# A three-layer decoder on one core, with the steps of its five queues in another order

## The reference

```python
x = x + _L0_attn_ref(_layernorm(x, axis=-1), L0_attn_wq, L0_attn_wk_down, L0_attn_wv_down, L0_attn_wk_up, L0_attn_wv_up, L0_attn_wo)
x = x + _L0_xattn_ref(_layernorm(x, axis=-1), ctx_768, L0_xattn_Wq, L0_xattn_bq, ...)
x = x + _L0_ffn_ref(_layernorm(x, axis=-1), L0_ffn_w1, L0_ffn_b1, L0_ffn_w2, L0_ffn_b2)
...
# feed-forward: bitlinear, exact gelu, bitlinear, where bitlinear(x, w, b) is
xn = rmsnorm(x)
xq = activation_quant(xn)      # scale 127 / max|xn|, round, clip
wq = weight_quant(w)           # scale 1 / mean|w|, round, clip to -1, 0, 1
return einsum('bsi,oi->bso', xq, wq) + b
```

## Time and profile before

| | |
|---|---|
| median of 3 runs | 320.35 us (320.17 to 320.55) |
| the profiled execution, its own time | 321.1 us |
| its span in the trace | 319.2 us |
| PE busy | 302.6 us, 95% |
| DVE busy | 273.2 us, 86% |
| ACT busy | 191.0 us, 60% |
| POOL busy | 161.5 us, 51% |

### The profile page before, as it was taken

How to read it: one execution, slowest core, us unless ns; L and a number is a source line. 1 busy time by engine, 2 the same in 40 slices (tenths; PEclk the granted TensorE clock), 3 DMA queues, 4 the chain that set the end, 5 groups by cost and what they waited for, 6 DMA issues and landing times.

```text
span 319.2 us, 8883 instructions
## 1 busy us (share of the span) xinstructions
PE 302.6 (95%) x3185; PEld 248.8 (78%) x3198; DVE 273.2 (86%) x488; ACT 191.0 (60%) x369; POOL 161.5 (51%) x315
## 2 busy tenths in 40 slices
PE   8798999999999999999999999999999999998756
PEld 8476787879888887897788878887887888786534
DVE  2228996898989799999999999989999998999973
ACT  3164435436247759478966854497445965776852
POOL 7337006282933523671778266306660485077873
PEclk9899999999999999999999999999999999999978
DMA  7999000000000000000001010000000010000011
GB/s 200 340 368 330 6 3 0 2 2 0 4 2 2 3 0 2 3 0 2 2 3 34 3 35 2 2 0 4 16 18 2 2 37 2 0 3 33 3 34 66
DMA packets 11954, 12.54 MB, mean 39 GB/s; under 512 B 1668, under 2 KB 11144, under 8 KB 11912
## 3 DMA queue, kind: packets, MB, share of 16 engines
q1 hardware_dynamic: 10648, 11.40, 10.9%
q10 hardware_dynamic: 1264, 0.59, 0.7%
HBM read 9.89 MB, written 2.10 MB: 38 GB/s over the span
## 4 chain that ended last, share of the span: by engine, by line
PE 77%; issue 6%; DVE 6%; POOL 5%; ACT 5%; DVEq 0%; POOLq 0%; ACTq 0%
PE bank L1724 8%; PE bank L1871 7%; PE bank L1804 6%; PE bank L1894 6%; PE bank L1822 6%; PE bank L1903 5%; PE quad L1784 4%; PE bank L1885 4%; PE bank L1730 4%; PE quad L1861 3%; PE bank L1942 3%; PE bank L1757 3%; PE bank L1718 2%; PE bank L1923 2%; PE bank L1932 2%
## 5 line engine op out<-in xcount | busy, mean ns | idle before, releaser
L845 ACT ACTIVATE c_p<-bank 77x512 f32<-77x512 f32 x64 | 35.7, 591 | 26.4 <-PE bank L1871 26.2
L1871 PE MATMUL bank<-ident,c_s 128*77 128x128 f32 x256 | 34.8, 274 | 0.4 <-DVE f_o L1369 0.4
L564 POOL TENSOR_SCALAR f_s<-f_mv 128x1 f32<-128x1 f32 x16 | 3.5, 220 | 62.0 <-DVE f_s L1325 61.4
L821 ACT ACTIVATE a_p<-bank 128x512 f32<-128x512 f32 x48 | 27.3, 601 | 10.5 <-PE bank L1804 10.1
L1894 PE MATMUL bank<-c_y,xw_s 128*128 128x128 f32 x256 | 31.5, 276 | 0.8 <-DVE c_y L1303 0.8
L1871 PEld LDWEIGHTS bank<-ident,c_s 128*77 128x77 f32 x256 | 29.5, 148 | 3.1 <-issue 1.0
L1894 PEld LDWEIGHTS bank<-c_y,xw_s 128*128 128x128 f32 x256 | 30.1, 192 | 1.3 <-issue 0.9
L1903 PE MATMUL bank<-xw_s,c_h 128*128 128x256 f32 x128 | 30.5, 381 | 0.0
L1273 DVE TENSOR_REDUCE c_nm<-quad 128x16 f32<-128x1232 f32 x16 | 23.0, 1436 | 4.2 <-PE quad L1861 4.1
L1903 PEld LDWEIGHTS bank<-xw_s,c_h 128*128 128x128 f32 x128 | 23.3, 190 | 3.6 <-ACT c_h L854 0.5
L1284 DVE TENSOR_TENSOR c_s<-quad,c_nm 128x616 f32<-128x616 f32 x32 | 24.5, 792 | 1.3
(11 more groups left out here) (139 smaller groups left out, 769.8 us busy)
## 6 DMA issues: line engine op xcount, KB each, us to landing
out<-f_o SPq DMA_DIRECT2D x16, 128.0 KB, 1.7
xres<-in_x SPq DMA_DIRECT2D x1, 1536.0 KB, 10.0
c_p<-in_wqT SPq DMA_DIRECT2D x2, 512.0 KB, 6.9
c_p<-in_wo SPq DMA_DIRECT2D x1, 1024.0 KB, 9.6
f_h<-in_fw1T SPq DMA_DIRECT2D x1, 1024.0 KB, 12.1
c_s<-in_fw2T SPq DMA_DIRECT2D x1, 1024.0 KB, 11.3
xw_s<-in_xw SPq DMA_DIRECT2D x2, 512.0 KB, 9.7
fb_s<-in_fb SPq DMA_DIRECT2D x1, 512.0 KB, 6.3
```

The lines of the kernel that those rows point to most:

```text
L821: nc.scalar.activation(dst, src, ACT.Exp, scale=SCALE_SA).then_inc(sa.sem["act"], 1)
L845: nc.scalar.activation(c_p[0:M, :, qt * P:(qt + 1) * P].rearrange("p (c j g) t -> p c j g t", c=KC, g=Q2)[:, :, j, :, :], bank("xs", f"tr{ ...
L1871: last = nc.tensor.transpose(dst[0:M, g * P:(g + 1) * P], c_s[:, qt, j, g, :], ident[:, :])
```

## The change

The change is in the order alone. Every step, every tile and every transfer is there as before, but the queues of all five engines list them in another order: the rows of `ORDER`, the calls at the end of each block, the list `EMPTIED` and SP's sixteen stores. The program's table was searched for with every hand-over between two engines taken longer than it was measured. The table's rows say little to a reader; here are its first ones on PE, and one piece each of what follows from it.

```diff
--- before.py
+++ after.py
@@ ORDER (one of its rows per engine) @@
 ORDER = dict(
     pe="""
-        pro.v3.0 pro.v1.0 pro.v2.0 sp.xT.0 pro.wq0.0 pro.wq1.0 pro.wqk0.0 pro.k1.0 pro.wqk1.0 sp.k.0 sp.q.0 sp.xT.1
-        sa.suA.0 pro.v0.0 pro.k3.0 sp.k.1 sp.v.0 sa.suB.0 pro.wvo.0 sp.xT.2 sp.q.1 sa.trA1.0 sa.trA0.0 sp.k.2
...
+        pro.wq0.0 sp.xT.0 pro.wq1.0 pro.wqk0.0 pro.v3.0 pro.wqk1.0 sp.k.0 sp.q.0 pro.v2.0 pro.k3.0 sa.suA.0 pro.k2.0
+        pro.k1.0 pro.v1.0 sp.v.0 sa.suB.0 sp.xT.1 sa.trA1.0 sa.trA0.0 pro.v0.0 sp.q.1 sp.k.1 sa.trB0.0 sa.trB1.0
...
@@ EMPTIED: the same pairs, in the order in which PE first comes to them @@
-    ("pro", "v3"): ("dve", ("v3",)),
-    ("pro", "v1"): ("dve", ("v1",)),
-    ("pro", "v2"): ("dve", ("v2",)),
+    ("pro", "wq0"): ("act", ("wq0",)),
     ("sp", "xT"): ("act", ("xT",)),
-    ("pro", "wq0"): ("act", ("wq0",)),
...
@@ SP's stores @@
+            f2_store(0, 1)
             f2_store(0, 0)
-            f2_store(0, 1)
...
@@ POOL's calls @@
+            xp_rstd(0)
+            xp_norm(0)
             sp_rstd(3)
             sp_norm(3)
-            xp_rstd(0)
-            xp_norm(0)
```

More of the change, by code:

```diff
@@ L173 @@
[L173 to L176 removed]
+        sp.norm1.1 sp.veps.2 sp.rstd.2 sp.norm0.2 sp.norm1.2 xp.veps.0 xp.rstd.0 xp.norm0.0 xp.norm1.0 sp.veps.3
@@ L177 @@
+        f2.hr0.7 f2.ht0.7 f2.ham0.7 f2.hinv0.7 f2.hqs0.7 f2.ms1.7 f2.hr1.7 f2.ht1.7 f2.ham1.7 f2.hinv1.7 f2.hqs1.7
+        f1.fb2.7 f2.hsc0.7 f2.hsc1.7
     """,
```

1561 lines of the change are left out of this document (780 added, 781 removed).

## The result

The new order takes 325.96 us (median of 4 runs, 325.31 to 326.80), before took 320.45 (320.17 to 322.09) beside it: ratio 1.0163, 95% interval 1.0121 to 1.0204. It is 5.5 us slower; I had forecast 1.4 us slower and a range that ended at 324.6. The profiled execution is 325.86 us long with a span of 323.9, so 4.7 us of span against the 319.2 of before have to be found.

The account below looks back on a forecast made before the run. PE paces the middle, DVE the fourteen us from 290, a chain of short steps the last fifteen. 2.4 - 0.6 - 2.65 + 1.72 - 0.3 + 0.84 = +1.4 us on 320.35 gives 321.7 us; range 318.4 to 324.6.

Parts of the forecast that it names:

- I count that as 0: End, POOL: fb2.7 no longer last, but out1.7 needs PE's last product and could not have been earlier; 0 us.
- at no difference: End, PE: the clock is low in this stretch before and will be again; no cost.
- three signs of being wrong: Head's clock stays high; PE's middle idles over 3 us or under 1; DVE no longer full from 290 us.
- The head, +2.4: PE's start: idle some 4.7 us ahead of wq0, then 5.4 us at half speed; +2.4 us, bounds -0.1 and 5.1.
- 1.48 us of PE work behind: Head, at suB.0: besides coming 0.96 us later, the new order has done 1.48 us less PE work.
- The rival that the clock comes back at once: Head costs -0.1 us and not 2.4, time 319.3 us; clock full before about 13 us; chance 0.12.
- The middle, -0.6: 32 to 290 us: a quarter of PE's 2.37 us of waits saved, as shortest distances grow; -0.6 us, ends -2.4 and +2.4.
- The table loads, 0: ACT's queue: two more loads, 2.6 us (5.3 with the skill's 2.66 us per switch), hidden by PE's work; 0 us.
- The lead, -2.65: Ahead of PE's xo.pv1.7: two steps fewer, f2.l20.4 and xm.w10.7, so element 7 gets there 2.65 us earlier.
- DVE's backlog, +1.72 - 0.3: DVE from xo.T1.7 to the last h: 1.72 us more work, 0.3 us of it filling idle time.
- The two `hsc`, +0.54: End, POOL: element 6's two hsc, 0.27 us each, stand ahead of sc1.7 and move every later step; +0.54 us.
- Both `hmax` behind the last `h`, +0.3: End, DVE: POOL's ht0.7 needs the first hmax, so tile 1's POOL steps start 2.7 us behind the last h; +0.3 us.

Follow-up runs that it names:

- warm_head: The new order with 34 multiplications of ones at the start of PE's queue instead of 12; 324.71 us, ratio 1.0118.
- end_new: Before's order up to T1.7, the last cross-attention output on DVE, and the new order behind it on every queue; 326.45 us, ratio 1.0172.
- before_fixed: Before with DVE's element 2 statistics behind the first maxima and subtractions, and multiplications of ones ahead of both wq (4, 3) and hT1.6 (12); 321.17 us, ratio 1.0006.

## Why the prediction was wrong

The direction was right, and so was the shape of the end (DVE full behind 290 us, a later last `h`, a longer chain). The time was 4 us short and out of the range. Up to `xo.pv1.7` the forecast was right by luck: head and middle together were to cost 1.8 us and cost 1.8, but as -0.3 and +2.1 and not as +2.4 and -0.6, so that `pv1.7` ended at 286.9 us, where the terms put it at 286.8. Of the 3.3 us that are missing between the 1.4 of the sum and the 4.7 of the span, 2.8 lie behind the last `h` and 0.5 in DVE's backlog. **The steps that failed are the two that were put at nothing there:** `fb2.7`'s place ("I count that as 0") and the low clock ("at no difference"). None of the three signs of being wrong came (the head's clock did fall, the middle's idle time was 2.62 us, DVE had 13.47 busy us of fourteen), since none of them watched the chain behind the last `h`. By its steps:

- *The head, +2.4: wrong.* The idle time (5.05 us for the 4.7 I took) and the clock at 0.50 came. But the clock was back at 14.2 us, 3.8 us behind the restart, not 5.4, and it cost about 1.2 us (warm_head), not 2.7. Before's own low stretch, which I gave its full 1.65 us, costs next to nothing by suB.0: end_new has the same head without it, is 1.71 us earlier at `sp.q.0`, but only 0.28 at suB.0 and suB.1, and its `wq0` started 0.27 us earlier anyway. before_fixed, with a full clock there, is not faster than before. What stands between is the wait for DVE's last subtraction, which ends at 24.96 us in end_new and at 25.25 in before: PE is idle for 2.50 us there and for 1.09. Here are `sp.q.0` and `suB.0` in end_new, beside 17.24 and 25.34 in before:

```profile
15.45 1.97 PE L1724 MATMUL bank<-a_xT,wqk 128*128 128x256 f32 x8
...
25.06 1.15 PE L1784 MATMUL quad<-a_k,a_q 32*128 32x256 f32 x16 [2.50 <-issue]
```

  For the same reason "1.48 us of PE work behind" was there (1.1 us at suB.0) but came with a step reached 1.1 us earlier. The rival that the clock comes back at once had the better size for the head (-0.1), though the clock was not back before 13 us, as it asked.
- *The middle, -0.6: wrong in sign.* It loses 2.1 us by the count of work. The 2.37 us that were "there to be had" were 1.4, as thirteen records were missing. Of the 2.1 us some 1.3 are idle time of PE: in after six waits of 0.29 to 0.72 us make up 2.5 of the 2.6 us, ahead of `xp.xT.0`, `w20.6`, `su0.4`, `l1_1.2`, `so.wo.4` and `su1.4`. The other 0.8 us sit inside steps that ran longer than usual. Counting the shortest distances told nothing of it.
- *The table loads, 0: nothing seen.* Each of the 42 loads in the two traces takes 1.283 us, and where an operation follows at once it starts 0.01 us behind the load. So no run shows the further time that the prediction quotes for a switch.
- *The lead, -2.65: right,* eaten by the middle.
- *DVE's backlog, +1.72 - 0.3: right in kind, 0.5 too small.* From `pv1.7` to the last `h` it is 2.4 us against the 1.96 of the forecast with the two `hsc`. A part is seen at 286.49: L1322 took 0.88 us where it takes 0.35, beside L551 (from 285.94 to 287.22), and T1.7 stood behind it.
- *The two `hsc`, +0.54: 0.45 came, by luck.* The two took 1.03 us and not 0.54, since they ran beside `hq1.6`; but `sc1.7`, which stood there in before and took 0.82 us, took 0.26.
- *Both `hmax` behind the last `h`, +0.3: 0.7.* The POOL steps of tile 1 start 2.8 us behind the last `h`, as forecast (2.7). The rest is L602's 0.90 us beside `hq0.7`.
- *"I count that as 0", of `fb2.7`'s place: wrong,* 0.9 us. I looked at who waits for the step, and not at what runs beside it.
- *"PE's clock is low in this stretch before and will be again, at no difference": wrong,* 1.5 us. Before gets the clock back at 313.67, ahead of its last two products; after had it at 0.50 until past 320, over both of them. With the head's 1.2 us the low clock costs 2.8 us in all, 0.9% of the span: the estimate of under 1% that I had from the Trainium skill (TensorE: Matmul & The Clock Gate, Part 1) holds, and yet it is more than half as large as the difference between the two orders. The same low stretch is free over steps that nobody waits for, and makes a step of the chain nearly twice as long (1.01 for 0.61 us, 3.62 for 2.07).

That the order's search counted longer hand-overs played no part that a run here could show. What stays open: what in the new order brings the middle's six waits and its longer steps. Moving the waiting steps only moved the waits. In after VectorE loses 6.1 us to instructions that grew beside GpSimd's, in before 4.0 (the sum over L1299, L1322, L1331 and L1357 of what is above the usual length); ahead of 286 us it is 4.33 against 3.35, so 1.0 us of the difference sits in the middle, but no run isolated what it costs. The head in its own right is open too, as told above.
